# Four layers on one core: a decay made one step earlier on ScalarE, and the carry of a scan kept by ScalarE in place of VectorE

## The reference

```python
# first layer, first block: a state space scan, 256 channels x 16 states
Bm = x @ W_B.T + b_B ;  Cm = x @ W_C.T + b_C
Delta = softplus(x @ W_Delta.T + b_Delta + bias_Delta)        # one step size a position
A_bar = exp(A * Delta) ;  B_bar = 1 / A * (A_bar - 1) * Bm
state = state * A_bar + x * B_bar ;  y = sum over states of state * Cm
x = layernorm(x + y)
# first layer, second block: 32 routed experts of which 8 are taken, and a shared one
aff = sigmoid(x @ Wr + br) ; the 8 largest, divided by their sum
x = layernorm(x + shared(x) + sum_e w_e * (silu(x @ Wg_e + bg_e) * (x @ Wu_e + bu_e)) @ Wd_e + ...)
# second layer, first block: input projection, causal convolution of 4 taps, silu, then a scan
dA = exp(dt * A) ;  h = dA * h + (dt * u) * B_t ;  y_t = sum over 16 states of h * C_t
x = layernorm(x + ((y + u * D) * silu(res)) @ out_w)
# second layer, second block: 16 experts of which 2 are taken for each of 8 heads
```

## Time and profile before

| | |
|---|---|
| median of 3 runs | 3472.85 us (3467.34 to 3473.31) |
| the profiled execution, its own time | 3465.27 us |
| its span | 3463.2 us |
| granted TensorE clock, mean | 0.954 |
| first layer, chunks 0 and 1 | 0 to 254.5 us |
| first layer, six chunks with tiles and experts | 254.5 to 1360 us |
| first layer's end and the way to the second | 1360 to 1669.1 us |
| second layer's scan | 1669.1 to 2640.1 us |
| second layer's experts | 2640.1 to 3463.2 us |

### The profile page before, as it was taken

One profiled execution on the slowest core, in us unless ns is written; L12 is line 12 of the kernel. 1 busy time (PEld: TensorE's weight loads), 2 busy tenths in 40 slices (PEclk: granted clock), 3 DMA queues, 4 the chain that ended last, 5 costly groups with the idle time before them and its releaser, 6 DMA issues. The chain is left out here.

```text
span 3463.2 us, 39510 instructions
## 1 busy us (share of the span) xinstructions
PE 3088.8 (89%) x11504; PEld 1701.8 (49%) x11504; DVE 2662.4 (77%) x3783; ACT 2282.6 (66%) x3239; POOL 2355.2 (68%) x1680
## 2 busy tenths in 40 slices
PE   3589999999999999998889999999976799999998
PEld 1156676666666667775334443443422333333332
DVE  5989898888988897554799999999996444544443
ACT  2457666666667666664666567666643488888887
POOL 3578888888888887773587888788783144444443
PEclk7689999999999999999899999999998799999999
DMA  2034444444444444553122222222221122222222
GB/s 94 13 97 128 122 128 126 127 121 119 131 123 121 124 120 130 146 148 87 61 68 70 71 69 69 71 70 68 71 70 55 53 99 99 105 105 104 103 101 86
DMA packets 199618, 335.38 MB, mean 97 GB/s; under 512 B 21379, under 2 KB 57380, under 8 KB 199020
## 3 DMA queue, kind: packets, MB, share of 16 engines
q1 hardware_dynamic: 199404, 332.86, 32.1%
HBM read 325.69 MB, written 7.09 MB: 96 GB/s over the span
## 5 line engine op out<-in xcount | busy, mean ns | idle before, releaser
L1435 POOL TENSOR_TENSOR c_hc<-c_h,c_c_rep 128x1024 f32<-128x1024 f32 x256 | 602.8, 2358 | 208.2 <-DVE c_h L1486 150.6
L1916 POOL TENSOR_TENSOR d_acc<-d_acc,d_prod 128x512 f32<-128x512 f32 x240 | 318.6, 1328 | 473.6 <-DVE d_prod L1984 473.2
L1486 DVE TENSOR_TENSOR_SCAN c_h<-c_decay,c_carry,c_v_ps 128x512 f32<-128x512 f32 x512 | 628.5, 1263 | 0.0
L1876 ACT ACTIVATE d_hmid<-d_up,d_b 128x1024 f32<-128x1024 f32 x512 | 539.7, 1112 | 78.4 <-PE d_up L1777 78.0
L1336 ACT ACTIVATE c_decay<-c_dt,c_a_cols 128x512 f32<-128x512 f32 x512 | 356.6, 718 | 337.0 <-DVE c_h L1486 319.9
L1186 PE MATMUL c_y_ps<-c_hc,ident 128*128 128x512 f32 x1024 | 507.1, 619 | 68.1 <-POOL c_hc L1435 56.1
L704 POOL TENSOR_TENSOR ab_inner_low<-ab_inner,ab_inner_high 128x512 fp32r<-128x512 f32 x264 | 341.1, 1292 | 239.5 <-ACT ab_inner_high L570 236.5
L559 ACT ACTIVATE ab_gate_ps<-ab_gate_ps,ab_raw_d 128x512 f32<-128x512 f32 x264 | 174.3, 660 | 445.7 <-PE ab_gate_ps L411 445.2
L1984 DVE SCALAR_TENSOR_TENSOR d_prod<-d_eo,d_b,d_w_rep 128x512 f32<-128x512 f32 x240 | 180.2, 751 | 314.9 <-PE d_eo L1787 172.8
L686 POOL TENSOR_TENSOR ab_hc<-ab_h,ab_c_rep 128x512 f32<-128x512 f32 x256 | 330.9, 1293 | 74.4 <-DVE ab_h L767 69.6
L1777 PE MATMUL d_up<-d_heads,d_w 128*128 128x512 f32 x1024 | 335.4, 434 | 16.6 <-ACT d_hmid L1876 9.4
(11 more groups left out here) (239 smaller groups left out, 6585.8 us busy)
## 6 DMA issues: line engine op xcount, KB each, us to landing
ab_raw_gu<-in_b_experts SPq DMA_DIRECT2D x264, 256.0 KB, 3.5
ab_w_rep<-ab_w_scratch SPq DMA_DIRECT2D x264, 256.0 KB, 3.7
c_c_rep<-c_c_scratch SPq DMA_DIRECT2D x256, 256.0 KB, 3.2
d_w_rep<-d_w_scratch SPq DMA_DIRECT2D x256, 256.0 KB
ab_raw_d<-in_b_experts SPq DMA_DIRECT2D x264, 129.0 KB, 2.1
ab_raw_x<-in_xT SPq DMA_DIRECT2D x32, 256.0 KB, 4.7
out<-xT SPq DMA_DIRECT2D x8, 512.0 KB, 3.4
xT<-in_xT SPq DMA_DIRECT2D x1, 3072.0 KB, 12.6
```

Source lines behind the costliest of these rows:

```text
L1435: nc.gpsimd.tensor_tensor(hc[:, q % HC], h[:, q % HR], c_rep[:, q % BC].unsqueeze(1).broadcast_to([P, PAIR, CH]), ALU.mult).then_inc(hc_re ...
L1486: nc.vector.tensor_tensor_scan(out=h[:, q % HR, m, :], data0=decay[:, i % DEC, :], data1=v_ps[m][:], initial=carry[:, i:i + 1], op0=ALU.mu ...
L1876: nc.scalar.activation(hmid[:, (2 * q + r) % HM], up_ps[r][:], ACT.Gelu, bias=b1[:, e:e + 1]).then_inc(gelu_ready, 1)
L1916: nc.gpsimd.tensor_tensor(acc[:, s, g, :], acc[:, s, g, :], prod[:, q % PR, :], ALU.add).then_inc(add_ready, 1)
```

## The change

First layer: the decay is made by a function of its own, `decay_of`. In step n ScalarE makes the decay of tile n + 1 in place of that of tile n; the decay of tile 0 is made ahead of the first chunk, and for a later chunk at the end of step 32 of the iteration before. In step 31 none is made. Second layer's scan: VectorE no longer keeps the last states. ScalarE copies them, for unit q - 4 in unit q, behind the two decays of q (in the first four units of a chunk those of the last four units of the chunk before). The first scan of a unit now waits for the copy of four units before, the unit whose slot of `h` it takes.

```diff
@@ scalar engine, first layer
+            def decay_of(c, s, n):
+                if n == 0:
+                    act.wait_ge(step_part, c * 3 + 3)
+                act.wait_ge(h_ready, c * NT + n + 1)
+                nc.scalar.activation(decay[:, n % AB, :], step[:, s, :], ACT.Exp,
+                                     scale=a_cols[:, n:n + 1]).then_inc(decay_ready, 1)
...
             def iteration(i, s):
                 for n in range(STEPS):
                     g = expert_at(i, n)
-                    if n < NT and below(i, NCH):
-                        if n == 0:
-                            act.wait_ge(step_part, i * 3 + 3)
-                        act.wait_ge(h_ready, i * NT + n + 1)
-                        nc.scalar.activation(decay[:, n % AB, :], step[:, s, :], ACT.Exp,
-                                             scale=a_cols[:, n:n + 1]).then_inc(decay_ready, 1)
+                    if n + 1 < NT and below(i, NCH):
+                        decay_of(i, s, n + 1)
...
+                    if n == NT and below(i, NCH - 1):
+                        decay_of(i + 1, 1 - s, 0)
...
             log_step(0)
+            decay_of(0, 0, 0)
@@ scalar engine, second layer's scan
+            def keep_last_states(c, q):
+                act.wait_ge(h_ready, c * NT + (q + 1) * PAIR + DEC)
+                nc.scalar.copy(carry[:, q * PAIR:(q + 1) * PAIR], h[:, q % HR, :, CH - 1]).then_inc(carry_ready, 1)
...
+                    if q >= HR:
+                        keep_last_states(c, q - HR)
+                    elif not first:
+                        keep_last_states(c - 1, NU - HR + q)
@@ vector engine, second layer's scan
-                    dve.wait_ge(carry_ready, c * NU + q + 1)
+                    dve.wait_ge(carry_ready, c * NU + q + 1 + NU - HR)
...
-            def keep_last_states(c, q):
-                dve.wait_ge(h_ready, c * NT + (q + 1) * PAIR + DEC)
-                nc.vector.reduce_max(carry[:, q * PAIR:(q + 1) * PAIR], h[:, q % HR, :, CH - 1:CH], axis=AX_X
-                                     ).then_inc(carry_ready, 1)
...
                     product(c, s, q)
-                    if q >= 1:
-                        keep_last_states(c, q - 1)
-                    elif not first:
-                        keep_last_states(c - 1, NU - 1)
                     scan(c, q, 0)
```

## The result

The changed kernel took 3422.05 us (median of 4 runs, 3419.13 to 3423.49) beside 3470.10 for the kernel before on the same chip (4 runs, 3461.08 to 3473.31): a ratio of 0.9869, 95% interval 0.9850 to 0.9887. On the 3472.85 us shown above that is 3427 us, 3421 to 3434. The forecast was 3428.

The account below looks back on a forecast made before the run. VectorE was taken to bound the second layer's scan and, through waits on ScalarE's decay and tanh, to stop PE in the first layer. Gains 21.7 + 8.1 + 15.3 = 45.1 us took 3472.85 to 3428, range 3415 to 3440.

Parts of the forecast that it names:

- The decay, 21.7 us: First layer: decay a step earlier gains 3.1 us a chunk, 18.5 in six, plus 3.2 in the first two chunks.
- the smaller of the decay wait and the time by which the tanh was early: First layer, steps 10, 16, 31: the gain per place, counted 0.82, 0.82 and, with a decay's 0.63 us, 1.45 us.
- The early chunks: First layer's first two chunks, before experts begin: nearly all of 3.3 us of decay waits goes, counted 3.2 us.
- The clock, 8.1 us: First layer: PE's shorter stops end nine clock falls at 0.9 us each; bounds 0 and 15.3 us.
- The carry, 15.3 us: Second layer's scan: 255 reduces leave VectorE at 0.062 us each, 15.8 us, bounds 10 and 17, less 0.5 for GpSimd.
- GpSimd's `dtu`: Second layer, chunk start: VectorE's faster last units run into waiting for this product, about 0.5 us lost once.
- ScalarE's copy: Second layer's scan: 252 copies add 18 to 144 us to ScalarE, hidden because it runs four units ahead; counted at nothing.
- PE takes the first layer back: Rival: first layer, VectorE's earlier arrival becomes longer tanh waits; gain only 15 to 25 us, 3448 to 3458; chance 0.15.
- The waits go whole: Rival: first layer, decay waits vanish entirely as the tanh doesn't stop VectorE; gain 86 us, 3387; chance 0.08.
- Table loads: Rival: second layer's scan, each small copy brings table loads on ScalarE; slower, about 3566 us; chance 0.04.
- Nothing: Rival: the reduce was hidden in the pipeline and PE takes the decay's gain; 3466 to 3480 us; chance 0.03.

Follow-up runs that it names:

- step 31 undone: Changed kernel with the decay of tile 31 made again at the head of step 31, behind the norm's Ln; 3433.31 us, one time.
- the carry alone: Kernel before with only the second layer's part, the carry copies moved to ScalarE; 3452.28 us, ratio 0.9965 to the kernel before.
- the double up product: Kernel before with PE's up product of steps 17 and 31 done twice, same values written again; 3456.72 us, ratio 0.9977 to the kernel before.
- four copies: Changed kernel with three more copies to an unread tile before each of ScalarE's carry copies; 3428.32 us, one time.
- the decay alone: Kernel before with only the first layer's part, the decay made a step earlier; 3436.82 us, ratio 0.9921 to the kernel before.
- the two steps: Changed kernel with the decay behind the bias and tanh at steps 10 and 16 only; 3423.51 us, ratio 0.9876 to the kernel before.
- every step: Changed kernel with the decay behind the bias and tanh in every step; 3428.47 us, ratio 0.9896 to the kernel before.
- one tap less: Changed kernel without the second of the convolution's four taps from the second chunk on; 3421.67 us, one time.
- the routing's new form: Changed kernel with the routing's sum as scalar_tensor_tensor and its four products as one tensor_tensor; 3423.48 us, ratio 0.9873 to the kernel before.
- the new form added: Changed kernel with the decay behind the tanh at steps 10 and 16 and the routing rewritten without tensor_scalar; 3418.91 us, ratio 0.9864 to the kernel before.

## Why the prediction was right

**The decay, 21.7 us.** Step by step the rule "the smaller of the decay wait and the time by which the tanh was early" held. At step 10 the wait left was put at 2.1 us and is 2.02 in the trace's count, 2.10 from start to start; at step 16 1.2 against 1.08 (1.16); at step 31 2.1 against 1.96 (2.04). Undoing step 31 alone cost 1.4 to 1.5 us a chunk, its term being 1.45. The tanh waits were to grow to some 55 us and are 57.3. The five chunks are 24.65 us shorter; without the 9.3 of the clock that is 15.4, against 5 x 3.1 = 15.5. The early chunks were to give 3.2, and the third begins 3.2 us sooner, but this agreement is not shown to be the decay's doing. The first chunk is 0.8 us shorter, as its decay wait is (8.0 to 7.1). The second is 2.65 shorter, and with the carry alone, with the decay where it was, it was 3.2 shorter too.

**The clock, 8.1 us.** No falls are left. PE's stops were put at 0.8 and 1.9 us and are 0.86 and 1.61. A fall was taken at 0.9 us between 0 and 1.7; the double up product gives 1.0 and step 31 undone 1.0 to 1.3. So the term was a little small, 9.3 us by the double up product, and the price lies within its bounds. That all nine falls went is in part luck: of the stops of 2.07 to 2.10 us in the later traces two of six had a fall, and the changed kernel's one of 2.07 had none. Up to the second layer's scan the two terms had 29.8 us and the trace has 30.35.

**The carry, 15.3 us.** The mechanism held and the size was off. From products to scan a unit lost 660 - 594 = 66 ns, so 255 x 0.066 = 16.8 us, at the upper of the two values weighed. The scan got 11.6. The step that failed is the one that names what is late next: it counted 0.5 us for GpSimd's `dtu` at a chunk's start, once, and nothing for PE. GpSimd took 0.4 more (0.9 us instead of 0.5). The rest is PE at units 13 to 15 and at units 4 to 13 of the first chunk, which VectorE's 3.54 us a unit has passed: 3.7 us more late products in all. Some of these 3.7 may be the copy's doing on ScalarE, up to the 1.9 us that follow from four copies. Another 0.9 us lies between the starts of the two scans of a unit, 1191 ns apart instead of 1187, for no cause that the runs show. 16.8 - 3.7 - 0.9 is 12.2, and 0.6 stays unaccounted. The prediction had PE's 872.75 of 971 us before it, and didn't ask which units PE filled.

ScalarE's copy was counted at nothing between 18 and 144 us of hidden work. It takes 252 x 0.094 = 24 us of ScalarE, and the scan never waits for a carry. The Trainium skill ("Perfetto Trace Analysis", Optimizing Scalar/DVE Operations) puts a small operation on SBUF at about 60 ns of VectorE and 93 of ScalarE, with profiled durations about twice as long. The trace agrees with both: 66 ns against a duration of 149 for the reduce, 94 against 186 for the copy.

**The rivals.** "PE takes the first layer back" is refuted by the decay alone, with 27 us, and by the five chunks, 24.6 us shorter. "The waits go whole" is refuted by the 57.3 us of tanh waits. "Table loads" by the 22 loads before the decays with one copy and with four. "Nothing" by the carry alone. Between the two profiled executions lie 41.8 us where the sum had 45.1: the first layer gave 0.6 more than counted, the second layer 3.7 less. The ratio of the timed runs, with 45.5 us and its interval from 39 to 52, can't tell these apart. That the forecast of 3428 meets 3427 to a microsecond is therefore luck: the intervals alone are 13 us wide. The bounds named for the range, 0 and 15.3 for the clock and 10 and 17 for the reduce, give gains of 31 to 54 us with the other terms, so 3419 to 3442, and not the 58 to 33 that were written beside it; the result lies in both.

## What to carry to other kernels

When two results of one engine are awaited one behind the other, moving the first ahead gains only up to the slack of the second: read from the trace by how much the second was early, step by step, and sum that. A small operation is worth the distance between the starts of its neighbours and not its duration, and whatever it uncovers, the next engine has to keep up unit by unit, so list that engine's fullest units and not its mean share. A stop of the matrix engine can cost twice, once as time and once as clock, and filling it with useless matmuls is a quick way to price the second.

## What the runs showed of the hardware

**VectorE and GpSimd get in each other's way over SBUF, for some operations.** In the changed kernel the routing's tensor_tensor on 128x128 (L837, both inputs in SBUF) took about 0.8 us in six of its eight executions, and each time ended 0.15 us after a GpSimd tensor_tensor that had started before it. The sum, a tensor_scalar of four columns (L831), took 0.44 us and ended 0.03 after GpSimd's operation:

```profile
878.74 0.74 POOL L704 TENSOR_TENSOR ab_dn_low<-ab_raw_d,ab_dn_high 128x256 fp32r<-128x256 f32 x1
879.07 0.44 DVE L831 TENSOR_SCALAR ab_total<-ab_total 128x4 f32<-128x4 f32 x1
...
883.86 1.30 POOL L692 TENSOR_TENSOR ab_hc<-ab_h,ab_c_rep 128x512 f32<-128x512 f32 x1
884.49 0.81 DVE L837 TENSOR_TENSOR ab_rest<-ab_aff,ab_rest 128x128 f32<-128x128 f32 x1
```

In the kernel before, the tensor_tensor took 0.28 us in the six full chunks, with GpSimd idle, and the sum 0.87 to 0.89, ending 0.02 us after a GpSimd operation. In the same chunk the sum took 1.17 us with the two steps and 0.32 with every step, again ending 0.03 us after GpSimd's. Where VectorE's tensor_tensor started 0.05 us before GpSimd's (884.20 before 884.25, in the rows of the kernel with the two steps) it took 0.28 us, and GpSimd's 1.38 instead of 1.29, 0.09 more although the two overlap for 0.23. Where it started only 0.02 us before (at 1241.62 in the same kernel), it took 1.47 us and ended 0.15 after GpSimd's. In the same stretches the operations with an input in PSUM (L805, 0.69 us) and the match_replace8 (0.17 to 0.18 us) had one length beside GpSimd's work and without it. The Trainium skill ("SBUF — State Buffer", SBUF: two separate sides) says that VectorE, in an operation with two SBUF inputs (against a GpSimd operation that reads SBUF) or in a two-port mode, and GpSimd share a pair of ports that the one to start first holds for its whole instruction. For VectorE's waits the trace agrees, with the numbers above; GpSimd's own delay was shorter than the overlap. By it, time won ahead of such an operation is given back if it then meets GpSimd's work, and this is what became of the gain at step 16 in three of the experiments.

**The clock after PE's stops.** These are the stops of PE of more than 1.4 us in the first layer's six chunks with tiles and experts, from 240 us on, in the twelve traces, and whether the clock fell there. Before: four of six stops of 2.5 us and five of five of 2.27. The carry alone: four of six and four of five. Step 31 undone: three of five of 2.27, and the one of 2.10. The changed kernel has one stop of 2.07 us, at step 18 of its last chunk, without a fall. The same stop has none at 2.10 us with the decay alone, at 2.08 with four copies and at 2.10 with one tap less, and has one at 2.09 us with the routing's new form. The decay behind the tanh at two steps makes it 2.80 us, without a fall, and with the new form added 2.79, with one. After none of the 76 shorter stops, up to 1.89 us, did it fall. What decides between two stops of the same length, no run here shows.

**Where two runs of the same code differ.** The first scan tile of the first layer starts between 39.3 and 43.4 us in the traces, whatever the edit. The second chunk takes 121.5 to 125.9 us, and 122.6 and 125.8 in two traces with the same code there. What follows the second layer's scan, which no edit touches, takes 817.8 to 826.2 us. So an edit that is worth 3 us is read from the lengths of the chunks or of the scan that it touches, and not from one time.
